# Layer 0 of a two-layer graph network: the third round of products is moved ahead of the next tile's third score group

## The chip, the cores and the metric

The kernel runs on one core of one Trainium2 chip. The metric is the device time of one execution in microseconds (us), as the median of several runs.

## The reference

3125 nodes with 1024 values each, 50000 edges sorted by their target `dst`, two layers. Layer 0 is an attention over the edges with 4 heads of 256 values, and the change lies in it alone:

```
xp = (relu(layernorm(x)) @ W).reshape(N, 4, 256)
a_src = einsum('nhc,hc->nh', xp, att_src);  a_dst = einsum('nhc,hc->nh', xp, att_dst)
# every node also has an edge to itself
e = leaky_relu(a_src[src] + a_dst[dst], 0.2)
ee = exp(e - segment_max(e, dst)[dst])
out = segment_sum(xp[src] * (ee / segment_sum(ee, dst)[dst]), dst)
x = x + relu(out + bias)
# then layer 1: layernorm, relu, one product with its W, and a second sum over edges
```

## The kernel before

The kernel first sorts the edges into lists and computes `xp` (lines up to 850), then runs `attend` (layer 0's sum over edges), then layer 1. `attend` goes over 25 tiles of 128 target nodes. A tile's edges are gathered from DRAM as rows of 1028 floats: 1024 of `xp` and 4 source scores. A tile has 18 gathers of up to 128 rows in five rounds, c = 0 to 4: four gathers in each of the first four rounds and two in the last. A buffer named `ring` holds two tiles.

For each round c of tile t the engines do this:

- GpSimd (POOL), line 1037: it issues the gathers of round (t, c), in order. It first waits until TensorE has consumed round (t-2, c), which lies in the same place (`ring_free`).
- ScalarE (ACT): `keep_edges` (line 1049) copies the 4 scores of each gathered row once they have landed, and `keep_scores` (line 1055) copies the turned scores back from PSUM.
- TensorE (PE): `turn(t, c)` (line 1113) transposes the scores of a round; `widen(t, c)` (lines 1124 and 1129) spreads them over the tile's nodes: one matmul with 128 rows of weights, then 8 matmul instructions with 16 rows of weights (8 in the last round). A turn and a widen of a round are called its score group here.
- VectorE (DVE): `highest_of(t, c)` (line 1251) takes the maximum over what `widen` wrote. There are two buffers `wide`, so `widen(t, c)` waits for the maximum two rounds back (`maxed`).
- PE: `add_rows(t, c)` (line 1173) is a round of products: 32 matmul instructions of 256 columns with 128 rows of weights (16 in the last round) that multiply the gathered rows by the weights of their edges and sum them by target node. Its last one signals `ring_free`.

PE's program interleaves two tiles: the products of tile t with the scores of tile t+1. The rounds of products are written out by hand between score groups (lines 1181 to 1208). After the fifth score group come the fourth round of products, `look_up` (line 1149), `spread_places` (lines 1139, 1141) and the fifth round.

VectorE finishes tile t-1 in between. After `highest_of(t+1, 1)` come `divide` (line 1312) and `finish` (lines 1318, 1321, 1322, ending in `mv_l`), and only then `highest_of(t+1, 2)`. ScalarE's program has `deviate(t-1)` (line 1070, it waits for `mv_l`) ahead of `keep_edges(t+1, 4)` and `keep_scores(t+1, 3)`, and PE's `turn(t+1, 4)` waits for `turned_kept` of round 3. SyncE (SP) issues for each tile four transfers of 512 KB or so: the rows of the tile itself, `x`, and the two results.

Of the kernel before, what the change touches and what calls it, by code (L numbers as in the profile page):

```python
# [850 lines left out]
def attend(nc, x, bias, va_d, list_d, table0, table1, x1_d, al_d, ident,  # L851
           idx0, idx0_last, idx0_first, idx0_last_first, loc0, loc0_last, a_src, a_dst, iota, nid, near16):
    RING = 2 * RC
    with ExitStack() as ctx:
# [102 lines left out]
        def blocks(c):  # L957

            return slice(OWN * QW, BLOCKS) if c == OWN else slice(c * QW, (c + 1) * QW)
# [148 lines left out]
        def _(pe):  # L1108
            def turn(t, c):
                n = H * (QW if c < OWN else QP)  # L1110
                pe.wait_ge(edge_a_done, RC * t + c + 1)
                pe.wait_ge(turned_kept, RC * t + c)
                pe.transpose(turned[0:n, 0:P], edge_a[:, blocks(c), :].rearrange("p q h -> p (q h)"), ident[:, :])\  # L1113
                    .then_inc(turned_done, 1)

            def widen(t, c):
                r = RC * t + c
                n = H * (QW if c < OWN else QP)
                to_nodes = spread if c < OWN else spread_last
                if c == 0:  # L1120
                    pe.wait_ge(absent_done, 2 * t + 2)
                if r >= 2:
                    pe.wait_ge(maxed, r - 1)
                pe.matmul(wide[r % 2][:, :, :], ident16[:, :],
                          absent[:, c * P:(c + 1) * P].rearrange("p (o s) -> p o s", o=1).to_broadcast([P, H, P]),
                          start=True, stop=False, skip_group_check=True)
                pe.wait_ge(turned_kept, r + 1)
                for h in range(H):
                    last = pe.matmul(wide[r % 2][:, h, :], to_nodes[:, h, :], score_T[0:n, c, :], start=False, stop=True,  # L1129
                                     skip_group_check=True)  # L1130
                last.then_inc(wide_done, 1)

            def spread_places(t):

                if t >= 1:
                    pe.wait_ge(maxed, RC * t)
                g, j = divmod(QW * t, WIN)
                nodes = of_tile[g * WIN:(g + 1) * WIN, j // QW, :]
                pe.matmul(wide[0][:, :, :].rearrange("p a s -> p (a s)"), nodes,
                          near16[g * WIN:(g + 1) * WIN, 0:OWN * P], start=True, stop=True)  # L1140
                pe.matmul(wide[1][:, 0, :], nodes, near16[g * WIN:(g + 1) * WIN, OWN * P:CAP], start=True, stop=True)\
                    .then_inc(places_spread, 1)

            def look_up(t):
                pe.wait_ge(member_done, t + 1)
                pe.wait_ge(lookup_done, t + 1)
                for c in range(RC):
                    q = slice(0, QW) if c < OWN else slice(QW, QW + QP)
                    last = pe.matmul(looked[:, blocks(c), :].rearrange("p q k -> p (q k)"), member[:, c * P:(c + 1) * P],
                                     lookup[:, q, :].rearrange("p q k -> p (q k)"), start=True, stop=True)  # L1150
                last.then_inc(looked_up, 1)

            def add_weights(t):

                pe.wait_ge(e_done, t + 1)
                pe.wait_ge(onehot_done, 2 * t + 2)
                for c in range(OWN):
                    pe.matmul(sums, onehot[:, c, :], e[:, blocks(c), :].rearrange("p q h -> p (q h)"),
                              start=c == 0, stop=False)
                pe.matmul(sums.rearrange("p (k o h) -> p k o h", k=QP, h=H), onehot[:, OWN, :],  # L1160
                          e[:, blocks(OWN), :].rearrange("p k (o h) -> p k o h", o=1).to_broadcast([P, QP, QW // QP, H]),
                          start=False, stop=True).then_inc(summed, 1)

            def add_rows(t, c):
                r = RC * t + c
                if c == 0 and t >= 2:
                    pe.wait_ge(acc_read, t - 1)
                pe.wait_ge(weighed, r + 1)
                q, n = (QW, WIN) if c < OWN else (QP, PAIR)
                by = weight[:, c, :].rearrange("p (q h n) -> p q h n", q=q, h=H)  # L1170
                for h in range(H):
                    for k in range(q):
                        last = pe.matmul(acc[t % 2][k * n:(k + 1) * n, h, :], by[:, k, h, :],  # L1173
                                         ring[:, t % 2, blocks(c), h * C:(h + 1) * C][:, k, :],
                                         start=c == 0 and h % 2 == 0, stop=c == RC - 1, skip_group_check=True)
                last.then_inc(ring_free, 1)
# [8 lines left out]
            for t in range(TILES):  # L1185
                more = t + 1 < TILES
                if more:
                    turn(t + 1, 0)
                add_rows(t, 0)
                add_weights(t)  # L1190
                if more:
                    turn(t + 1, 1)
                    widen(t + 1, 0)
                add_rows(t, 1)
                if more:
                    turn(t + 1, 2)
                    widen(t + 1, 1)
                    turn(t + 1, 3)
                    widen(t + 1, 2)
                add_rows(t, 2)  # L1200
                if more:
                    turn(t + 1, 4)
                    widen(t + 1, 3)
                    widen(t + 1, 4)
                add_rows(t, 3)
                if more:
                    look_up(t + 1)
                if t + 2 < TILES:
                    spread_places(t + 2)
                add_rows(t, 4)  # L1210
# [1982 lines left out]
```

## Time and profile before

| | us |
|---|---|
| median of 3 runs | 2069.11 |
| lowest and highest | 2063.67, 2078.47 |
| the profiled execution | 2064.15 |
| its span | 2060.0 |

Busy time as a share of the span: PE 84%, POOL 49%, DVE 60%, ACT 22%. The mean granted clock of TensorE over the run is 0.849 of full speed. `attend` lies in the span from about 510 to 1320 us. Times of an instruction are counted from the span's start. "Busy" counts the time of instructions; ends of matmuls are modelled. "PEclk" is the clock granted to TensorE, where 1.00 is 2.4 GHz and 0.50 is 1.2 GHz. "DMA share" is the mean busy share of the 16 DMA engines. A bracket at the end of a row is the idle time of its engine just before it, and what ended it.

### The profile page before, as it was taken

What the parts mean: (1) busy time and instruction counts of PE and PEld (TensorE: products, weight loads), DVE (VectorE), ACT (ScalarE), POOL (GpSimd) and SP (SyncE); (2) the same over time, 40 slices, a digit from 0 to 9 for tenths busy, and PEclk for the clock granted to TensorE, in tenths of its full rate; (3) what the DMA queues carried; (4) which work ended last, traced back from release to release, by engine and by line L of the source; (5) the groups of instructions that cost most, each with busy time, mean ns of one, the idle gap of its engine ahead of it and who ended that gap; (6) DMA issues with size and microseconds to landing.
All of it is one profiled execution on the core that took longest, in us unless ns stands there. A gap on an engine that the chain in (4) does not pass through costs nothing. (4 is left out here: it accounts for less than half of the span.)

```text
span 2060.0 us, 28377 instructions
## 1 busy us (share of the span) xinstructions
PE 1720.9 (84%) x10668; PEld 949.9 (46%) x10668; DVE 1233.4 (60%) x2867; ACT 460.9 (22%) x893; POOL 1013.7 (49%) x935
## 2 busy tenths in 40 slices
PE   4897999886288888989999988158999989999896
PEld 2443444443155555555555555114554445544454
DVE  4999999987157777776777777433233233333332
ACT  3332333221012221221222122112122112222221
POOL 1011111011746676666777761176676666666740
PEclk9898999897567678777777778568999999999998
DMA  7221323221969999999999994299999999999971
GB/s 231 91 91 56 99 76 105 84 85 63 407 223 340 352 356 378 342 343 351 356 357 367 371 356 134 106 411 381 344 358 362 342 345 361 343 371 355 354 246 47
DMA packets 170578, 553.19 MB, mean 269 GB/s; under 512 B 32195, under 2 KB 37178, under 8 KB 170080
## 3 DMA queue, kind: packets, MB, share of 16 engines
q0 software_dynamic: 128128, 416.72, 55.3%
q1 hardware_dynamic: 38708, 121.44, 17.3%
q10 hardware_dynamic: 3600, 13.16, 1.7%
q8 instruction: 87, 1.43, 0.3%
q14 instruction: 55, 0.45, 0.1%
HBM read 546.15 MB, written 53.45 MB: 291 GB/s over the span
## 5 line engine op out<-in xcount | busy, mean ns | idle before, releaser
L1037 POOL DMA_INDIRECT ring<-layer_rows,idx x360 | 401.5, 1115 | 213.7 <-PE acc L1173 93.7
L1631 POOL DMA_INDIRECT ring<-layer_rows,idx x360 | 368.8, 1024 | 182.6 <-issue 93.3
L560 PE MATMUL mm<-w_sb,hT 128*128 128x512 f32 x800 | 361.6, 606 | 0.0
L1173 PE MATMUL acc<-ring,weight 128*32 128x256 f32 (+1 forms) x3600 | 344.7, 506 | 6.8 <-issue 3.9
L446 POOL DMA_INDIRECT src_lists<-run,starts x28 | 55.5, 1983 | 398.8 <-DVE run L787 390.5
L1693 PE MATMUL acc<-ring,weight 128*32 128x512 f32 x1600 | 212.2, 617 | 38.6 <-ACT weight L1641 19.2
L560 PEld LDWEIGHTS mm<-w_sb,hT 128*128 128x128 f32 x800 | 152.8, 196 | 174.1 <-issue 174.1
L1173 PEld LDWEIGHTS acc<-ring,weight 128*32 128x32 f32 (+1 forms) x3600 | 154.4, 143 | 143.7 <-issue 108.5
L1793 DVE TENSOR_TENSOR hT_low<-tp_l,hT_high 128x512 fp32r<-128x512 f32 x50 | 34.6, 692 | 299.4 <-issue 237.2
L1726 PE MATMUL mm_l<-w_high,hT_high 128*128 128x512 f32 x400 | 170.3, 426 | 10.6 <-issue 8.4
L1251 DVE TENSOR_REDUCE highest<-wide 128x4 f32<-128x512 f32 x125 | 85.2, 681 | 146.9 <-PE wide L1129 76.5
L1727 PE MATMUL mm_l<-w_low,hT_high 128*128 128x512 f32 x400 | 163.2, 408 | 8.7 <-issue 8.5
L1728 PE MATMUL mm_l<-w_high,hT_low 128*128 128x512 f32 x400 | 163.2, 408 | 7.6 <-issue 7.5
L1129 PE MATMUL wide<-score_T,spread 16*128 16x128 f32 x800 | 137.8, 320 | 0.1
L1129 PEld LDWEIGHTS wide<-score_T,spread 16*128 16x128 f32 x800 | 115.9, 219 | 40.4 <-issue 37.9
L1693 PEld LDWEIGHTS acc<-ring,weight 128*32 128x32 f32 x1600 | 45.2, 110 | 149.1 <-issue 149.0
L1726 PEld LDWEIGHTS mm_l<-w_high,hT_high 128*128 128x128 f32 x400 | 77.9, 195 | 68.4 <-issue 51.3
L743 DVE TENSOR_TENSOR_SCAN running<-mine,nought 100x1792 f16<-100x1792 f16 x28 | 108.8, 3887 | 1.0
L1641 ACT ACTIVATE weight<-weight 128x128 f32<-128x128 f32 x125 | 38.6, 309 | 301.0 <-issue 181.3
L1113 PE MATMUL turned<-ident,edge_a 128*16 128x128 f32 (+1 forms) x125 | 38.3, 307 | 78.0 <-ACT score_T L1055 31.5
L1728 PEld LDWEIGHTS mm_l<-w_high,hT_low 128*128 128x128 f32 x400 | 78.0, 195 | 30.0 <-issue 12.1
L1727 PEld LDWEIGHTS mm_l<-w_low,hT_high 128*128 128x128 f32 x400 | 78.3, 196 | 28.3 <-issue 13.3
(264 smaller groups left out, 2374.7 us busy)
## 6 DMA issues: line engine op xcount, KB each, us to landing
layer_rows<-row_l ACTq DMA_DIRECT2D x25, 514.0 KB, 3.8
layer_rows<-row_l SPq DMA_DIRECT2D x25, 514.0 KB
own<-layer_rows SPq DMA_DIRECT2D x25, 512.0 KB
x<-xb SPq DMA_DIRECT2D x25, 512.0 KB
x1t<-x SPq DMA_DIRECT2D x25, 512.0 KB
xt<-in_x_dram SPq DMA_DIRECT2D x24, 512.0 KB
xb<-in_x_dram SPq DMA_DIRECT2D x24, 512.0 KB
out_dram<-y SPq DMA_DIRECT2D x24, 512.0 KB
```

The source lines that it names most:

```text
L446: pool.indirect_dma_start(out=list_d, out_offset=bass.IndirectOffsetOnAxis(ap=starts[:, c:c + 1], axis=0), in_=run[c % 2][:, :], in_offset ...
L560: last = pe.matmul(mm[k][:, f * HALF:(f + 1) * HALF], hT[k][:, c, :], w_sb[:, c, f * HALF:(f + 1) * HALF], start=c == 0, stop=c == KC - 1)
L743: then(dve.tensor_tensor_scan(running[:, :], mine[c % 2][:, :], nought[0:NWP, 0:1].to_broadcast([NWP, CW]), 0.0, ALU.add, ALU.max), scanned)
L1037: pool.indirect_dma_start(out=ring[:, t % 2, blocks(c), :][:, q, :], out_offset=None, in_=table0, in_offset=bass.IndirectOffsetOnAxis(ap=i ...
L1129: last = pe.matmul(wide[r % 2][:, h, :], to_nodes[:, h, :], score_T[0:n, c, :], start=False, stop=True, skip_group_check=True)
L1173: last = pe.matmul(acc[t % 2][k * n:(k + 1) * n, h, :], by[:, k, h, :], ring[:, t % 2, blocks(c), h * C:(h + 1) * C][:, k, :], start=c == ...
L1251: then(dve.tensor_reduce(highest[:, c, :], wide[r % 2][:, :, :], AX_X, ALU.max), maxed)
L1631: pool.indirect_dma_start(out=fetched(t, c)[:, q, :], out_offset=None, in_=table1, in_offset=bass.IndirectOffsetOnAxis(ap=idx, axis=0), bo ...
L1693: last = pe.matmul(acc[t % 2][q * wide:(q + 1) * wide, f * HALF:(f + 1) * HALF], weight[t % 2][:, c, q * wide:(q + 1) * wide], fetched(t, ...
L1726: pe.matmul(mm[:, cols], hT_high[:, c, :], w_high[:, c, cols], start=c == 0, stop=False)
L1727: pe.matmul(mm[:, cols], hT_high[:, c, :], w_low[:, c, cols], start=False, stop=False)
L1728: last = pe.matmul(mm[:, cols], hT_low[:, c, :], w_high[:, c, cols], start=False, stop=c == KC - 1)
```

## The change

In each tile's part of PE's program, `add_rows(t, 2)` stood behind the third and fourth turn and the second and third widen of the next tile; now it stands behind the third turn and second widen. `turn(t+1, 3)`, `widen(t+1, 2)`, `turn(t+1, 4)`, `widen(t+1, 3)` and `widen(t+1, 4)` then follow with no products between them. No instruction is added or removed, and no other engine's program is touched.

```
                 if more:
                     turn(t + 1, 2)
                     widen(t + 1, 1)
+                add_rows(t, 2)
+                if more:
                     turn(t + 1, 3)
                     widen(t + 1, 2)
-                add_rows(t, 2)
-                if more:
                     turn(t + 1, 4)
                     widen(t + 1, 3)
                     widen(t + 1, 4)
```

## Rows read from the trace of the kernel before

**Rows 1.** The page's first line: the span of the profiled execution

```profile
span 2060.0 us, 28377 instructions
```

**Rows 2.** Busy time by stretch: PE, PEld, DVE, ACT, POOL; PEclk, DMA share, GB/s

```profile
620.00:1240.00 620.00, 556.93 (x4528) 331.33 (x4532) 448.32 (x1070) 132.69 (x336) 425.76 (x375) 0.75 0.98 355
820.80:851.85 31.05, 28.76 (x216) 17.10 (x216) 21.60 (x51) 6.40 (x17) 19.95 (x18) 0.70 0.96 349
942.54:973.91 31.37, 27.57 (x216) 16.62 (x216) 21.50 (x52) 6.30 (x17) 20.66 (x18) 0.73 0.96 346
912.84:942.54 29.70, 27.84 (x216) 16.14 (x216) 21.66 (x52) 6.31 (x17) 20.35 (x18) 0.71 0.98 353
1061.16:1090.10 28.94, 27.57 (x216) 16.06 (x216) 21.31 (x51) 6.32 (x17) 21.02 (x18) 0.71 0.99 355
```

**Rows 3.** Timeline of VectorE: `highest_of` of round 1, tiles 3 and 23

```profile
645.79 0.69 DVE L1251 TENSOR_REDUCE highest<-wide 128x4 f32<-128x512 f32 x1 [2.51 <-DMA edge_pack<-tail_pack]
...
1236.79 0.69 DVE L1251 TENSOR_REDUCE highest<-wide 128x4 f32<-128x512 f32 x1 [2.29 <-issue]
```

**Rows 4.** Timeline of all engines between the second maximum and `turn(t+1, 4)`, tile 9

```profile
820.80 0.69 DVE L1251 TENSOR_REDUCE highest<-wide 128x4 f32<-128x512 f32 x1 [1.14 <-DMA edge_pack<-tail_pack]
821.11 0.37 PE L1113 MATMUL turned<-ident,edge_a 128*16 128x128 f32 x1 [3.16 <-ACT score_T L1055]
...
826.33 0.21 DVE L1322 BATCH_NORM_AGGREGATE mv_l<-stats_l 128x2 f32<-128x12 f32 x1
...
826.87 0.25 ACT L1055 ACTIVATE score_T<-turned 16x128 f32<-16x128 f32 x1
...
827.41 0.38 PE L1113 MATMUL turned<-ident,edge_a 128*8 128x128 f32 x1
...
827.78 0.99 POOL L1037 DMA_INDIRECT ring<-layer_rows,idx  x1 [0.78 <-PE acc L1173]
```

**Rows 5.** Timeline of POOL, tile 9: the gathers after the fourth round of products

```profile
836.58 0.98 POOL L1037 DMA_INDIRECT ring<-layer_rows,idx  x1 [3.51 <-PE acc L1173]
...
851.86 0.99 POOL L1037 DMA_INDIRECT ring<-layer_rows,idx  x1 [1.29 <-PE acc L1173]
```

**Rows 6.** Timeline of POOL: the same first gather after the fourth round, tiles 13 and 17

```profile
958.22 0.99 POOL L1037 DMA_INDIRECT ring<-layer_rows,idx  x1 [3.56 <-PE acc L1173]
...
1074.35 1.82 POOL L1037 DMA_INDIRECT ring<-layer_rows,idx  x1 [0.68 <-PE acc L1173]
```

**Rows 7.** Timeline of PE, tile 13: fourth turn, third round, fifth turn, fourth round

```profile
942.85 0.27 PE L1113 MATMUL turned<-ident,edge_a 128*16 128x128 f32 x1 [0.77 <-ACT score_T L1055]
...
944.35 1.93 PE L1173 MATMUL acc<-ring,weight 128*32 128x256 f32 x32
949.00 0.37 PE L1113 MATMUL turned<-ident,edge_a 128*8 128x128 f32 x1 [2.72 <-ACT score_T L1055]
...
954.27 3.64 PE L1173 MATMUL acc<-ring,weight 128*32 128x256 f32 x32
```

**Rows 8.** Timeline of PE, tile 17: the same four

```profile
1061.47 0.37 PE L1113 MATMUL turned<-ident,edge_a 128*16 128x128 f32 x1 [1.70 <-ACT score_T L1055]
...
1064.20 3.64 PE L1173 MATMUL acc<-ring,weight 128*32 128x256 f32 x32
1067.78 0.38 PE L1113 MATMUL turned<-ident,edge_a 128*8 128x128 f32 x1
...
1070.87 2.98 PE L1173 MATMUL acc<-ring,weight 128*32 128x256 f32 x32
```

**Rows 9.** Stretches of PE alone: busy time, PEclk, DMA share, GB/s

```profile
828.00:831.00 3.00, 3.00 (x11) 0.50 0.97 355
...
1061.50:1068.00 6.50, 6.50 (x44) 0.50 0.98 343
1068.50:1071.50 3.00, 3.00 (x29) 1.00 0.95 323
```

**Rows 10.** The same view, tile 13, just before the fifth turn

```profile
948.00:949.00 1.00, 0.00 (x0) 0.86 1.03 411
```

More of the change, by code:

```diff
@@ L1197, in _ @@
                     widen(t + 1, 1)
+                add_rows(t, 2)
+                if more:
                     turn(t + 1, 3)
                     widen(t + 1, 2)
-                add_rows(t, 2)
-                if more:
                     turn(t + 1, 4)
```

## The prediction

> **What bounds the kernel now.** I first read the busy time by stretch for `attend` [rows 2], then the timeline of VectorE for a mark that recurs once per tile [rows 3], then the timelines of PE, POOL and ScalarE between two marks [rows 4 to 8], and last the granted clock [rows 9, 10]. My mark is the start of `highest_of(t+1, 1)`, the maximum over the second score group. The 20 tiles from 645.79 to 1236.79 take 591.0 us, a mean of 29.55 us each [rows 3].
>
> Three things are nearly full there. The DMA share is 0.98 and PE is busy 556.93 of 620 us [rows 2]; POOL issues 18 gathers per tile. The share alone doesn't say who sets the pace: a period of 31.05 us has 0.96 at 349 GB/s, one of 28.94 us has 0.99 at 355 [rows 2]. The DMA engines have some room in the slow tiles and little in the fast ones.
>
> So I cut a period into three pieces, at `turn(t+1, 4)` and at the first gather that the fourth round of products releases.
>
> - Mark to fifth turn: 827.41 - 820.80 = 6.61 us [rows 4], 949.00 - 942.54 = 6.46 [rows 2, 7], 1067.78 - 1061.16 = 6.62 [rows 2, 8]. It is nearly fixed, because it is a chain of VectorE and ScalarE: the maximum, `divide` and `finish` up to `mv_l` at 826.33, the square root, then `score_T` of round 3 at 826.87, and `turn(t+1, 4)` waits for that [rows 4].
> - Fifth turn to that gather, x: 836.58 - 827.41 = 9.17 us [rows 4, 5], 958.22 - 949.00 = 9.22 [rows 6, 7], 1074.35 - 1067.78 = 6.57 [rows 6, 8]. This is PE's own work: two widens and a round of products.
> - That gather to the next mark: 851.85 - 836.58 = 15.27 [rows 2, 5], 973.91 - 958.22 = 15.69, 1090.10 - 1074.35 = 15.75 [rows 2, 6]. It hardly varies, though PE's clock does.
>
> Hence a period is about 6.5 + x + 15.5 us, and the tiles differ by x alone. From the mean of 29.55, the mean x is 7.55. What makes x 9.2 or 6.6 is the clock. A round of products lasts 1.93 us at 2.4 GHz and 3.64 at 1.2 GHz [rows 7]. Where x was 9.2, PE had 0.50 (1.2 GHz) while it widened [rows 9]; where it was 6.57, it had 1.00 from 1068.5 to 1071.5, just after a third round at 1064.20 to 1067.84 that filled the stretch at 0.50 before it [rows 8, 9]. In tile 13 the third round ran early and fast (944.35 to 946.28), PE then stood idle for 2.72 us, the clock fell within 948 to 949, and the widens and the fourth round ran at half speed: 3.64 us [rows 7, 10]. So products bring the clock up, and a stretch of idle time and widens takes it down.
>
> **The change, part by part.**
>
> *The third round earlier.* 32 matmuls and their weight loads go ahead of one turn and one widen. The work is the same. They no longer wait for ScalarE's `score_T` of round 2, and can start when the second widen is through. In tile 9 PE idled 3.16 us just there, in tile 13 0.77, in tile 17 1.70 [rows 4, 7, 8]. This idle time is not removed from the period: it reappears ahead of the fifth turn, which is still held by the 6.5 us chain. PE's work in that window is a round, a turn and a widen: 6.3 us when all is slow (821.11 to 827.41 [rows 4]), 946.28 - 942.85 = 3.4 when fast [rows 7]. Both fit in 6.5. Gain: nothing; at most the 0.15 us by which slow windows end at 6.61 instead of 6.46.
>
> *The turn and widen later* by one round, 1.9 to 3.6 us less the idle time that the round fills. Behind them: ScalarE's `keep_scores` of round 3, which has to wait for `mv_l` anyway, and VectorE's third maximum, which comes behind `mv_l`, 5.6 us past the mark. At the fast clock the widen ends 3.5 us past the mark, at the slow one about 6.3, so the maximum could start up to 0.7 late. It is not on the way to the fifth turn. I cost it at nothing; if that cover fails, 0.7 us in slow tiles.
>
> *`ring_free` of the third round earlier.* POOL's gathers of that round wait 0.78 us for it in tile 9 [rows 4]. That wait goes; 0 to 0.8 us per tile. What is late next is `ring_free` of the fourth round, for which POOL already waits 3.51 us in tile 9 [rows 5]; that wait only grows. The queue has the same transfers in the same order, and none is issued by PE; SP's four transfers per tile are issued behind VectorE's and ScalarE's work and don't move. At a DMA share of 0.98 an earlier issue lengthens a queue, and it could win back at most the idle share, (1 - 0.98) x 620 = 12 us. I take 0, since the wait that drains the queue is the one for the fourth round, which doesn't come earlier; the ends are 0 and -12.
>
> *The clock.* Here the change has a price. Up to now the third round stands directly ahead of the fifth turn and often raises the clock for the two widens and the fourth round. Afterwards the last products before the fifth turn end about 2 us past the mark (fast) and then come a turn, a widen, some 3 us idle, a turn and two widens. That is tile 13's pattern, with still more sparse work in it, in every tile. I expect the clock at 1.2 GHz through the fourth round in some two thirds of the tiles (x = 9.2) and for the rest a little of 2.4 GHz at the start of the widens (x about 8.1, halfway from 7 to 9.2): a mean of 8.8. From below, x stays at 7.55; from above, 9.2. Per tile (8.8 - 7.55) = +1.25 us; over the 22 periods in which `attend` is in this rhythm, +27.5 us; the ends are 0 and 22 x 1.65 = +36.
>
> The Trainium skill ("TensorE: Matmul & The Clock Gate", section "HAM oscillation — how this bites in real kernels") holds idle gaps of PE against the clock and would have them closed. By that rule the change helps at one gap and harms at another. Its section "Part 1: The HAM clock gate" has activity release the throttle. The trace agrees only in part: from 828 to 831 PE was busy for 3.00 of 3.00 us, with widens, and stayed at 0.50 [rows 9]. By the page the busy widens should do as well as products; by the row they don't.
>
> **The sum** is against the profiled execution, 2064.15 us (span 2060.0 [rows 1]): 2064.15 + 27.5 = 2091.7. That execution lies 5 us below the median of the runs shown (2069.11) and near their lowest, so on the median's level the sum would be 2096.6. I put 2093.
>
> **The rivals.**
>
> 1. *The clock doesn't care, or another resource paces the tiles.* Then x stays near 7.55, and only the earlier `ring_free` counts: 2064 to 2069, less up to 12 us. For it: the DMA share of 0.98. Against it: periods follow x to within half a us whatever the DMA share.
>
> 2. *Faster: the filled gap keeps the clock up.* The third round closes the 0.8 to 3.2 us of idle time behind the second widen, so the clock no longer falls there and holds through the widens. Then x is 1.93 for the round, 1070.87 - 1067.78 = 3.09 for the widens [rows 8] and some 0.3 for the signal: 5.3. That alone would be 22 x 2.2 = 49 us less, but the DMA engines moved 355 GB/s x 28.94 us = 10.3 MB in the fast tile at a share of 0.99 [rows 2], so I allow no period much below 28.6, which is 22 x 1 = 22 us less: 2042 to 2047. It decides if the clock at the fifth turn is 1.00 and stays there to the fourth round. Against it: tile 13. This is also where the skill's rule on gaps would lead.
>
> 3. *Slower still: the mark moves.* If the completion of the second widen is seen by VectorE only when the products queued behind it are through, `highest_of(t+1, 1)` starts 1.9 to 3.6 us later in every tile, and the 6.5 us chain starts from there: 22 x 1.9 = 42 to 79 us, 2106 to 2148. For it: in tile 9 PE's idle time begins at 821.11 - 3.16 = 817.95, with the modelled end of the second widen, and VectorE starts only at 820.80 [rows 4]: completion and model differ already. Against it: nothing in the order asks for it.
>
> **Chances.** Forecast 0.50 (its own range 2078 to 2108), first rival 0.25, faster 0.15, third rival 0.10. Around 1%, some 21 us, is what a measurement of this kernel can tell from no change; that is above 2089.8 or below 2048.4. Three quarters of the forecast's case and all of the third rival lie above: 0.38 + 0.10 = 0.48. Faster by over 1% is 0.15 with the second rival. The rest is 0.37. The range takes in the first rival and a part of the second, and leaves out the third: 2048 to 2112.
>
> **What would show it.** In the changed kernel: mark to fifth turn still 6.5 us, now with 2 to 4 us of PE's idle time ahead of the fifth turn and hardly any ahead of the fourth; x near 9 in most tiles, with fourth rounds of 3.64 us; POOL's wait for the third round gone and that for the fourth longer, 3 us and more in most tiles; the stretch from that gather to the next mark unchanged at 15.5; the DMA share down to 0.96. The period should be 30.5 to 31. The prediction fails if fourth rounds of 1.93 us become more frequent, if the mark lies a round behind the second widen, or if the 15.5 us piece changes, because it is only observed to be constant and I don't know which of its members holds it.

## The result and the profile after

The changed kernel takes 2103.72 us in the median of 4 runs (2094.23 to 2107.43), the kernel before 2073.79 (4 runs). The ratio is 1.0134, with a 95% interval from 1.0089 to 1.0179: slower, by about 1.3%. This ratio and those below are estimated from the executions and not from the two medians, whose quotient differs a little (here 1.0144). They leave out executions over 1.5% above the fastest of their kernel: nine of the eleven of the kernel before and one of the six with sparse fillers in the first set of experiments, and one of the twelve with fillers in two groups. The profiled execution took 2094.23 us, 30.1 more than that of before, and its span of 2092.3 us is 32.3 longer.

The stretch of `attend` after, with the columns of [rows 2], once as a whole and for one tile from mark to mark:

```profile
620.00:1260.00 640.00, 544.15 (x4437) 333.24 (x4438) 442.03 (x1055) 130.25 (x332) 413.75 (x372) 0.77 0.95 340
832.45:863.12 30.67, 25.75 (x222) 15.64 (x218) 21.32 (x51) 6.31 (x17) 20.64 (x18) 0.78 0.97 347
```

The DMA share fell from 0.98 to 0.95. The granted clock, averaged over the stretch, is 0.77 and was 0.75. So the mean clock is no lower; what matters is where in the tile it is low. The marks of tiles 3 and 23 after, which answer to [rows 3]:

```profile
647.06 0.69 DVE L1251 TENSOR_REDUCE highest<-wide 128x4 f32<-128x512 f32 x1 [2.29 <-PE wide L1129]
...
1265.54 0.69 DVE L1251 TENSOR_REDUCE highest<-wide 128x4 f32<-128x512 f32 x1 [0.70 <-issue]
```

20 tiles take 618.48 us, 30.92 each, where it was 29.55. Cut as in the prediction, with the means over these 20 tiles:

| us per tile | before | after |
|---|---|---|
| mark to fifth turn | 6.57 | 6.48 |
| x, fifth turn to the gather that the fourth round releases | 7.53 | 9.03 |
| that gather to the next mark | 15.45 | 15.42 |
| period | 29.55 | 30.92 |
| PE idle ahead of the fourth turn, of the fifth turn | 1.58, 0.66 | 0.00, 3.49 |

The whole difference is in x: it was 8.8 or more in 5 tiles of 20 and is now in all 20 (8.8 to 9.2). One tile of after, from its timeline of all engines, answers to [rows 4, 5, 7]:

```profile
832.18 1.67 PE L1173 MATMUL acc<-ring,weight 128*32 128x256 f32 x25 [0.31 <-issue]
...
832.45 0.69 DVE L1251 TENSOR_REDUCE highest<-wide 128x4 f32<-128x512 f32 x1 [2.51 <-PE wide L1129]
...
833.78 0.28 PE L1113 MATMUL turned<-ident,edge_a 128*16 128x128 f32 x1
...
838.52 0.25 ACT L1055 ACTIVATE score_T<-turned 16x128 f32<-16x128 f32 x1
...
838.91 0.37 PE L1113 MATMUL turned<-ident,edge_a 128*8 128x128 f32 x1 [3.55 <-ACT score_T L1055]
...
844.18 3.45 PE L1173 MATMUL acc<-ring,weight 128*32 128x256 f32 x32
...
847.94 1.03 POOL L1037 DMA_INDIRECT ring<-layer_rows,idx  x1 [3.38 <-PE acc L1173]
```

The third round is under way at the mark. The fourth turn and the third widen follow without a pause, PE stands idle for 3.55 us, and the fifth turn goes at 6.46 us past the mark, released by `score_T` as before. The fourth round then needs 3.45 us. PE's granted clock in the same tile (busy time, PEclk, DMA share, GB/s):

```profile
833.00:836.00 3.00, 2.36 (x26) 1.00 1.00 373
836.00:837.00 1.00, 0.00 (x0) 1.00 0.96 296
837.50:847.00 9.50, 8.09 (x47) 0.50 0.99 361
847.50:850.00 2.50, 2.50 (x24) 1.00 0.75 303
```

It falls in the idle time and comes back only when the fourth round is over: the two widens and the round, which make up x, run at 1.2 GHz.

### The profile page after: what moved, and what is told of

It is laid out like the page before. It is cut to its first block and busy times, and to the rows that moved or that the text cites. A ratio compares the mean times of both kernels' runs of the same rounds, so it can differ in the third digit from the quotient of the medians.

```text
span 2092.3 us, 28377 instructions
## 1 busy us (share of the span) xinstructions
PE 1718.2 (82%) x10668; PEld 956.4 (46%) x10668; DVE 1233.0 (59%) x2867; ACT 460.2 (22%) x893; POOL 1007.5 (48%) x935
## 5 line engine op out<-in xcount | busy, mean ns | idle before, releaser
L1173 PE MATMUL acc<-ring,weight 128*32 128x256 f32 (+1 forms) x3600 | 324.7, 477 | 10.3 <-DVE weight L1286 6.6
L1693 PE MATMUL acc<-ring,weight 128*32 128x512 f32 x1600 | 220.0, 620 | 44.0 <-issue 24.2
L1129 PE MATMUL wide<-score_T,spread 16*128 16x128 f32 x800 | 143.6, 330 | 0.0
L1129 PEld LDWEIGHTS wide<-score_T,spread 16*128 16x128 f32 x800 | 121.2, 228 | 42.5 <-issue 39.4
L647 DVE CUSTOM_DVE_ANT_0 prod<-row_l,att_bc 128x256 f32<-128x256 f32 x200 | 84.8, 424 | 9.0 <-ACT row_l L501 2.5
```

The costliest lines, as they stand in the source:

```text
L647: dve.tensor_tensor_reduce(out=prod[:, :], in0=row[k][:, h * C:(h + 1) * C], in1=att_bc[:, j, h * C:(h + 1) * C], scale=1.0, scalar=0.0, o ...
L1693: last = pe.matmul(acc[t % 2][q * wide:(q + 1) * wide, f * HALF:(f + 1) * HALF], weight[t % 2][:, c, q * wide:(q + 1) * wide], fetched(t, ...
```

## The experiments

The runs fell on three chips, one for each set of four. Each kernel is compared with the kernel before on its own chip. The means over 20 tiles are of tiles 3 to 22 of each trace, cut as above.

### The two kernels again, and more DMA traffic

> The kernel before, unchanged, for its profile on the chip of these runs: period = 6.5 + x + a third piece, with x between 6.5 and 9.2 from tile to tile. Its time should be within half a per cent of the kernel before.

> The changed kernel, unchanged, beside the kernel before on this chip. Clock theory: x of 8.8 to 9.2 in nearly every tile and 0.7 to 1.8% slower than before. If the third piece is shorter on a chip with faster memory, the loss is the same in us, 15 to 35. If the loss came from the DMA engines, it would vanish on such a chip.

The changed kernel with x1 stored twice:

```
                 sp.dma_start(rows(x1_d, t), xt[t % 2][:, :]).then_inc(x1_out[t % 2], 16)
+                sp.dma_start(rows(x1_more, t), xt[t % 2][:, :]).then_inc(x1_out[t % 2], 16)
```

> The changed kernel with each tile's x1 stored twice, the second time to a buffer that nobody reads: 512 KB more per tile, 5% more traffic. If PE's clock and the chain over the engines set the period in the changed kernel, the DMA engines have room (share 0.95): 0 to 0.4 us a tile, 0 to 10 us in all. If the DMA engines set it: 512 KB at 350 to 400 GB/s is 1.3 to 1.5 us a tile, 29 to 34 us.

| | median us | ratio to before | period, x, third piece |
|---|---|---|---|
| before, again | 2064.68 | 0.9992 (0.9962 to 1.0023) | 29.47, 7.51, 15.34 |
| after, again | 2086.36 | 1.0101 (1.0065 to 1.0137) | 30.63, 9.29, 14.88 |
| after, x1 stored twice | 2089.84 | 1.0096 (1.0061 to 1.0131) | 30.59, 9.26, 14.86 |

The loss repeats, and with it x. 5% more traffic changes neither the period nor the ratio. The busy time of the two from 640 to 1240 us, first of after again, then with x1 stored twice:

```profile
640.00:1240.00 600.00, 501.04 (x4187) 304.58 (x4187) 416.68 (x988) 124.97 (x313) 398.91 (x352) 0.78 0.96 343
```

```profile
640.00:1240.00 600.00, 500.57 (x4202) 306.80 (x4202) 418.93 (x996) 124.93 (x313) 395.90 (x351) 0.79 0.99 361
```

The engines moved 361 instead of 343 GB/s and their share rose from 0.96 to 0.99. They had that room, so they don't set the pace of the changed kernel. It also shows that a share near 1 is by itself no proof of a bound. The kernel before, at 0.98, did not run with more traffic.

### Fillers on PE: is it the clock, and what raises it?

Extra matmuls were put ahead of the fifth turn. They write to the buffer that `widen(t + 1, 3)` overwrites next, and nobody reads them. In the sparse kernel only the call differs: `fill(t + 1, 10, 16)`.

```
+            def fill(t, n, k=P):
+                pe.wait_ge(maxed, RC * t + 2)
+                for _ in range(n):
+                    pe.matmul(wide[(RC * t + 3) % 2][:, :, :].rearrange("p a s -> p (a s)"), ident16[0:k, :],
+                              absent[0:k, 0:OWN * P], start=True, stop=True, skip_group_check=True)
...
                     widen(t + 1, 2)
+                    fill(t + 1, 10)
                     turn(t + 1, 4)
```

> The changed kernel with 10 extra matmuls (bfloat16, 128 rows of weights, 512 columns, results never used) on PE between widen(t+1, 2) and turn(t+1, 4), where PE now stands idle for 3 to 4 us. Clock theory: they last 2.1 us at 2.4 GHz and fit into the idle time; they keep the clock up, the two widens and the fourth round run faster, x falls from 9 to between 5.3 and 7.5, the period from 30.9 to between 28 and 29.5, and the time to 2045 to 2070. If the order of the gathers or the DMA engines set the slower pace: no gain, 2094 to 2108. If the clock were low all the same, the fillers last 4.3 us and cost up to 3 us a tile: 2120 to 2170.

> The same 10 extra matmuls in the same place, with as many columns but only 16 rows of weights, like those of the widens. If only products with many rows raise the clock: it stays at 1.2 GHz there, x stays at 9, and the fillers at that clock last up to 4.3 us, some of it past the end of the idle time: 2100 to 2160. If it is idle time as such that lowers the clock, this kernel is as fast as the one with the dense fillers: 2045 to 2070.

And in the kernel before, between the third round and the fifth turn:

```
                 add_rows(t, 2)
                 if more:
+                    fill(t + 1, 6)
                     turn(t + 1, 4)
```

> The kernel before with 6 of the dense fillers between add_rows(t, 2) and turn(t+1, 4), where PE is idle for 0 to 2.7 us. Clock theory: 1.3 us at 2.4 GHz, tiles with x of 9.2 become rarer, mean x from 7.55 to 6.5 to 7: 2045 to 2062. If the clock isn't what differs between the tiles: 2069 to 2100, since in tiles without idle time the fillers only delay the fifth turn.

This first set ran on a chip where the kernel before takes 1980.64 us and its runs lie between 1943.96 and 1995.55. The dense fillers in the changed kernel took 1939.74 (ratio 0.9916, 0.9834 to 0.9999), the sparse ones 1960.73 (1.0034, 0.99 to 1.0169), the fillers in the kernel before 1937.16 (0.9909, 0.9841 to 0.9977). The mean x was 7.01, 8.99 and 5.80. With no profile of the two base kernels on that chip, and two executions of the kernel before behind the ratios, this was not conclusive, so the three ran again beside the changed kernel on a chip like the first.

> The changed kernel once more, as the base of this set, for the two kernels with fillers need it on the same chip. Clock theory: mean x 9.0 to 9.3; 0.7 to 1.5% slower than before. Its third piece is 14.9 to 15.4 us if the chip's memory is like the first one's, nearer to 13 if it moves 409 GB/s in layer 1.

> The changed kernel with the 10 dense fillers, now beside the changed kernel on the same chip. Clock theory: mean x 6.5 to 7.3 against 9 to 9.3, 1 to 2% faster than the changed kernel. If the fillers did nothing and the earlier gain was the chip: no faster than the changed kernel.

> The changed kernel with 10 fillers of 16 rows of weights, beside the dense ones on the same chip. If the rows count: mean x stays at 8.9 to 9.3, the time within 0.5% of the changed kernel and 1% or more over the dense fillers. If idle time alone lowers the clock: x and time as with the dense fillers.

> The kernel before with 6 dense fillers between the third round and the fifth turn. Clock theory: mean x 5.8 to 6.5, up to 0.7 us lost ahead of the fifth turn in tiles where the fillers don't fit, 0.5 to 1% faster than before. If it was the chip: within 0.3% of before.

| one chip; before 2078.57 us | median us | ratio to before | period, x, third piece |
|---|---|---|---|
| changed kernel | 2107.73 | 1.0156 (1.0113 to 1.0199) | 31.09, 9.24, 15.38 |
| + 10 dense fillers | 2068.87 | 0.9972 (0.9943 to 1.0002) | 29.52, 7.67, 15.39 |
| + 10 sparse fillers | 2112.28 | 1.0181 (1.0134 to 1.0227) | 31.57, 9.75, 15.35 |
| before + 6 dense fillers | 2052.84 | 0.9882 (0.9838 to 0.9927) | 29.64, 6.15, 16.37 |

The dense and the sparse kernel have the same instructions, columns and places, and PE is about as busy. From 640 to 1240 us, first dense, then sparse:

```profile
640.00:1240.00 600.00, 538.55 (x4569) 318.60 (x4582) 436.19 (x1038) 128.31 (x323) 415.88 (x365) 0.85 0.99 357
```

```profile
640.00:1240.00 600.00, 547.22 (x4283) 324.43 (x4274) 405.49 (x968) 120.11 (x302) 376.78 (x342) 0.76 0.94 334
```

PE was busy for 538.55 us with a mean clock of 0.85 in the one and for 547.22 with 0.76 in the other. The dense fillers take back 1.84% of the changed kernel's time (2107.73 to 2068.87), the sparse ones nothing. Mean x is above what was expected in both (7.67 for 6.5 to 7.3, 9.75 for 8.9 to 9.3): in two tiles of the dense kernel and five of the sparse one x is 11.1 to 11.4. Without these it is 7.3 and 9.2. One tile of the sparse kernel is shown further below. A tile of the dense kernel, PE's timeline, fillers first (ten are issued, the trace has nine):

```profile
734.51 2.11 PE L1167 MATMUL wide<-absent,ident 128*128 128x512 bf16 x9 [0.16 <-issue]
738.03 0.27 PE L1113 MATMUL turned<-ident,edge_a 128*8 128x128 f32 x1 [1.42 <-ACT edge_a L1049]
...
738.44 1.15 PE L1129 MATMUL wide<-score_T,spread 16*128 16x128 f32 x8
...
741.05 3.44 PE L1179 MATMUL acc<-ring,weight 128*32 128x256 f32 x32
```

And one of the sparse kernel:

```profile
747.74 2.32 PE L1167 MATMUL wide<-absent,ident 16*128 16x512 bf16 x10
751.26 0.37 PE L1113 MATMUL turned<-ident,edge_a 128*8 128x128 f32 x1 [1.20 <-ACT score_T L1055]
...
751.99 2.07 PE L1129 MATMUL wide<-score_T,spread 16*128 16x128 f32 x8
```

The fillers, the idle time and the turn are alike (mean idle time ahead of the fifth turn: 1.35 us with the dense fillers, 1.14 with the sparse ones); the widen that follows takes 1.15 us in one and 2.07 in the other. So the loss comes from the clock, and filling the idle time isn't enough to keep it up: ten matmuls with 16 rows of weights left x and the time where they were without them. What it is about 128 rows that counts, the rows themselves or how much of the array works, these runs don't separate. In the dense kernel the clock still falls within the widens or early in the fourth round, so the fourth round stays slow here, which is the main reason why x is 7.7 and not 5.3.

**A version that beats both.** The kernel before with six dense fillers is 1.18% faster than before (0.73 to 1.62%), and in the first set it was 0.91% faster (0.23 to 1.59%). Its profiled execution (2068.18 us) is the slowest of its six, so its pieces understate it. x is 6.15; part of it is given back, since the fillers delay the fifth turn to 7.12 us past the mark and the third piece is 16.37.

### Fillers in two groups

```
                     widen(t + 1, 2)
+                    pe.wait_ge(maxed, RC * (t + 1) + 2)
+                    fill(t + 1, 4)
+                    if t >= 1:
+                        pe.wait_ge(x1_done, t)
+                    fill(t + 1, 7)
                     turn(t + 1, 4)
```

Here `fill` has no wait of its own.

> The changed kernel with 11 dense extra matmuls before turn(t+1, 4), 4 of them after the second maximum and 7 only after x1 is written, some 4 us past the mark, so that they always end just ahead of the fifth turn. Clock theory: the clock is at 2.4 GHz at the fifth turn in nearly all tiles, x between 5.3 and 7 everywhere, mean idle time ahead of the fifth turn under 1 us; 10 to 20 us faster than the fillers in one block, and 1.5 to 3% below the kernel before. If something else bounds the tiles at about 28 us, x falls and the third piece grows by as much, and it is no faster than with the fillers in one block (about 1% below).

2059.65 us, ratio 0.9969 (0.9937 to 1.0002), so no difference from the kernel before is shown; period 29.24, x 6.76, third piece 15.94. The idle time ahead of the fifth turn is down to 0.63 us, as expected, and x fell by 2.5 us against the changed kernel on the same chip. Of these only 1.4 reached the period, because the third piece grew by 1.06. That is the second of the two expectations in its mechanism, but not in its time of about 1% below the kernel before. Whether two groups are better than one block isn't shown, since the two ran on different chips. On this chip hardly a tile goes below a period of 28.3 us, whatever x. In tiles with x of 6.0 the third piece was 15.7 to 20.0. The busy time from 640 to 1240 us:

```profile
640.00:1240.00 600.00, 543.03 (x4685) 317.14 (x4678) 439.07 (x1045) 129.16 (x328) 415.80 (x367) 0.87 0.99 359
```

The DMA share is back at 0.99, with 359 GB/s. The doubled store had room to use at a period of 30.6 us; nothing here excludes that the DMA engines hold the faster tiles near 28.3.

### What holds the third piece

```
                     widen(t + 1, 3)
-                    widen(t + 1, 4)
                 add_rows(t, 3)
                 if more:
+                    widen(t + 1, 4)
                     look_up(t + 1)
```

> The kernel before with the fourth round of products ahead of widen(t+1, 4) instead of behind it: it asks what holds the constant 15.5 us between the gather that the fourth round releases and the next mark. If it is POOL's own chain of ten gathers, everything from the gather on comes earlier by a widen, 1.5 to 2.6 us a tile: 2010 to 2040. If it is PE's and VectorE's chain through look_up, x falls by that much and the 15.5 piece grows by as much: 2060 to 2080.

2013.89 us, ratio 1.0306 (1.0229 to 1.0384), and 1.7% above even the median of all eleven executions of the kernel before, 1980.64: much slower, which neither expectation had. x is 6.13 and the third piece 18.83; the kernel before has no profile on this chip. PE's timeline of one tile:

```profile
787.69 3.33 PE L1173 MATMUL acc<-ring,weight 128*32 128x256 f32 x32
...
791.27 1.15 PE L1129 MATMUL wide<-score_T,spread_last 8*128 8x128 f32 x8
795.27 2.29 PE L1149 MATMUL small<-lookup,member 128*128 128x32 f32 x10 [2.85 <-DVE lookup L1263]
```

and POOL's of the same tile:

```profile
791.33 0.99 POOL L1037 DMA_INDIRECT ring<-layer_rows,idx  x1 [0.71 <-PE acc L1173]
...
801.66 1.09 POOL L1037 DMA_INDIRECT ring<-layer_rows,idx_last  x1 [5.45 <-PE acc L1173]
```

The gather came early and then POOL waited 5.45 us for the fifth round. So in this order POOL's chain of ten gathers does not hold the third piece. VectorE's chain from the fifth maximum to `lookup` does take part: its 2.6 us or so, which the fourth round can cover in the order of the two kernels, now stood bare ahead of `look_up`. What makes the piece 15.4 us in the order of the two kernels, and on the faster chip less (the sparse kernel: 13.48 there, 15.35 here), stays open.

## Why the prediction was right

*What bounds the kernel.* The cut held: 6.5, x, 15.4. Both outer pieces moved by less than 0.1 us in the change. The doubt about the DMA share was settled by the doubled store for the changed kernel, which is where the loss is; for the kernel before it stays.

*The clock term*, the only one that I gave a price. Mean x was predicted at 8.8 and is 9.03. Slow tiles were forecast to be two thirds, for which no row stood, and are all of them (in the two repeats x was below 8.8 in one tile of 40). The guess of two thirds was too low, but 8.8 and the upper end of 9.2 lie close together, so it cost little. The sum of +27.5 us compares with +30.1 between the profiled executions: 22 x 1.37 us of the longer period is that number. Taking 1.25 instead of 1.50 for x was a shade low, and the 0.09 us that the first piece gave back is the "at most 0.15" of the third round's term. The level was the larger error: 2093 forecast, 2103.72 measured, since the profiled execution of before lies near the fast end of its runs.

*What raises the clock* was told too simply. The working blames the slow tile 13, where PE stood idle ahead of the fifth turn, and concludes that products bring the clock up. But in tiles 9, 11 and 22, three of the five slow ones of the kernel before, the third round stood directly ahead of the fifth turn, with no idle time between. PE in tile 9 of the kernel before, and its stretch from the fourth turn to the end of the fourth round:

```profile
821.11 0.37 PE L1113 MATMUL turned<-ident,edge_a 128*16 128x128 f32 x1 [3.16 <-ACT score_T L1055]
...
823.84 3.64 PE L1173 MATMUL acc<-ring,weight 128*32 128x256 f32 x32
827.41 0.38 PE L1113 MATMUL turned<-ident,edge_a 128*8 128x128 f32 x1
...
832.68 3.58 PE L1173 MATMUL acc<-ring,weight 128*32 128x256 f32 x32
```

```profile
821.00:836.00 15.00, 14.89 (x93) 8.45 (x93) 10.89 (x26) 4.70 (x8) 9.46 (x8) 0.50 1.00 370
```

PE was busy for 14.89 of 15 us and a full third round passed, and the clock stayed at 0.50 to the end of the fourth. These three tiles share 2.7 to 3.2 us of idle time ahead of the fourth turn; but that isn't the answer either: in the repeat of the kernel before, tiles 9 and 22 have 2.85 and 3.04 us there and x is 6.40 and 7.54, while the five tiles with x of 8.8 or more have at most 1.69. So with a round directly ahead the clock is often up, not always, and what decides it in a tile stays open. The forecast holds because the change puts the idle time and the widens behind the last products in every tile.

*The earlier `ring_free`.* Priced at nothing. POOL's wait for the third round went from a mean of 0.64 us to 0.34, and that for the fourth grew from 1.90 to 4.04. The DMA share fell. Nothing of the 12 us came.

*The later turn and widen.* Priced at nothing, 0.7 us if the cover fails. In the profile after it held, but in a few tiles of other executions it did not: in the two repeats x was 10.1 to 10.8 in 5 tiles of 40. A tile of the sparse kernel shows what happens. `mv_l` was done at 812.57, yet VectorE's timeline has

```profile
815.47 0.69 DVE L1258 TENSOR_REDUCE highest<-wide 128x4 f32<-128x512 f32 x1 [2.90 <-DMA edge_pack<-tail_pack]
```

The third maximum waited 2.90 us for a widen whose modelled end lay before 810.2, and the matmuls with few rows of the fifth widen then came late by 1.85 us and more. VectorE's only wait there is for that widen; the DMA in the bracket is the profile's guess. That is 2 us in such a tile, three times the bound that I gave, but rare in the changed kernel.

*The rivals.* The first (no effect) and the second (faster, the filled gap keeps the clock up) are refuted by x and by the clock rows: the gap ahead of the fourth turn was filled completely, 1.58 us to 0.00, and the clock fell all the same one gap later. The third (the mark moves behind the products) is refuted by the tile above: the mark at 832.45 lies within the third round, which ran to 833.85.

*The skill's rule.* The section "HAM oscillation — how this bites in real kernels" of "TensorE: Matmul & The Clock Gate" in the Trainium skill speaks of idle gaps. The changed kernel agrees with it: 3.49 us of idle time ahead of the fifth turn, and the clock is low for most or all of x in every tile. The sparse fillers differ from it: they close the same gap as the dense ones, and the clock stays down. The measurement decides: to close the gap was not enough here, it took matmuls with 128 rows of weights. The row that the prediction set against the rule (828 to 831 us, widens, 0.50) bears less than it was given: the full third round just before it had not raised the clock either.

## What to carry to other kernels

When PE's work alternates between full matmuls and ones with few rows, the order of the two can decide the clock: try to have full matmuls directly ahead of the critical stretch, and check in the granted clock that it is up there, since one round alone did not always raise it. Look where the clock is low, not how low it is on average. Cut the period of a loop at the waits that hold it and see which piece differs between slow and fast tiles of the same trace; that piece is where a change can pay. A DMA share near 1 is not proof of a bound: double one transfer and look, in the kernel that the question is about.

## What was unexpected of the hardware

PE's work is sometimes seen as complete by VectorE, ScalarE and POOL at nearly the same moment and up to 3 us after its modelled end (2.90 us above; 2.85 in [rows 4]). In the kernel with x1 stored twice ScalarE waited for a turn that ended by the model at 913.22, VectorE for a widen that ended at 914.51 and POOL for a round of products that ended at 913.01:

```profile
916.43 0.27 ACT L1057 ACTIVATE score_T<-turned 16x128 f32<-16x128 f32 x1 [0.82 <-remote]
916.53 0.69 DVE L1253 TENSOR_REDUCE highest<-wide 128x4 f32<-128x512 f32 x1 [1.10 <-DMA edge_pack<-tail_pack]
916.63 0.99 POOL L1039 DMA_INDIRECT ring<-layer_rows,idx  x1 [1.13 <-remote]
```

What holds the completion back stays open. Six matmuls per tile whose results nobody reads made the kernel 1.2% faster. And the chips differ: the gathers of layer 1 ran at about 355 GB/s in the first two profiles and at 409 on the chip of the first set of fillers, where the kernel before took 1980.64 us instead of 2073.79. GB/s in 40 slices, of the changed kernel with dense fillers on that chip, then on the chip of the second set:

```profile
GB/s 242 82 97 63 91 83 112 79 92 73 160 410 372 347 382 360 389 369 359 371 382 389 372 380 302 99 214 410 409 409 409 410 409 408 408 409 408 409 246 50
```

```profile
GB/s 230 90 91 66 91 74 104 84 84 74 406 220 356 357 363 366 366 353 366 342 356 338 366 354 113 158 410 367 356 355 353 366 357 328 353 367 328 331 224 47
```
